# The next unit's first normalisation moved one iteration up, and the kept sums inverted tile by tile

## The reference

```
h = ln(x)*(1+sc)+sh ; windowed self attention (16 heads of 16, windows of 128, rolled by 64) ; x += g*(o @ w_so + b_so)
h = ln(x)*(1+sc)+sh ; scores = q @ k_ctx (77 context rows); top 16 of 77; softmax over them; x += g*(attn @ v @ w_co + b_co)
h = ln(x)*(1+sc)+sh ; u = h @ w_m1 ; x += g*((silu(u[:1024]) * u[1024:]) @ w_m2 + b_m2)
```

```
nx = ln(x)*gamma+beta ; w = softmax(nx @ Wq @ (bank @ Wk).T / 16) ; combined = [nx, w @ (bank @ Wv), anchor]
probs = softmax(combined @ router_W + b) ; 3 experts: silu(combined @ e_w1 + b) @ e_w2 + b, summed with probs
out = x + sigmoid(silu(combined @ gate_w1) @ gate_w2) * (routed @ out_w + out_b)
```

## Time and profile before

| | |
|---|---|
| median of 3 runs | 1451.67 us (1446.48 to 1452.09) |
| the profiled execution | 1447.34 us |
| its span, first to last instruction | 1445.5 us |
| PE busy | 97% of the span |
| DVE busy | 1061.5 us, 73% |
| ACT busy | 815.8 us, 56% |
| POOL busy | 439.9 us, 30% |
| mean granted TensorE clock | 0.992 |

### The profile page before, as it was taken

One profiled execution on the slowest core, in us unless ns is written; L12 is line 12 of the kernel. 1 busy time (PEld: TensorE's weight loads), 2 busy tenths in 40 slices (PEclk: granted clock), 3 DMA queues, 4 the chain that ended last, 5 costly groups with the idle time before them and its releaser, 6 DMA issues.

```text
span 1445.5 us, 29891 instructions
## 1 busy us (share of the span) xinstructions
PE 1402.6 (97%) x9585; PEld 1174.8 (81%) x9585; DVE 1061.5 (73%) x4754; ACT 815.8 (56%) x2523; POOL 439.9 (30%) x600
## 2 busy tenths in 40 slices
PE   7999999999999999999999999999999999999997
PEld 5878788888888788888888788888888878887886
DVE  3576869687786868879696787959688786968632
ACT  3473474747566375755647366564757547474433
POOL 1414132333224233332335132233334313232302
PEclk9999999999999999999999999999999999999999
DMA  7610000000010000010010000000010000000000
GB/s 244 207 64 2 1 8 19 9 27 9 20 32 16 1 2 25 1 34 9 19 33 1 16 1 16 11 23 13 8 34 19 16 2 7 3 1 9 1 2 14
DMA packets 32760, 35.29 MB, mean 24 GB/s; under 512 B 8744, under 2 KB 27868, under 8 KB 32349
## 3 DMA queue, kind: packets, MB, share of 16 engines
q1 hardware_dynamic: 32605, 33.38, 7.6%
HBM read 28.83 MB, written 4.22 MB: 23 GB/s over the span
## 4 chain that ended last, share of the span: by engine, by line
PE 59%; DVE 31%; issue 5%; ACT 2%; POOL 1%; SPq 0%; DMA 0%; DVEq 0%; POOLq 0%; ACTq 0%
PE bank L1033 10%; DVE knocked L2264 10%; PE bank L964 9%; PE bank L1009 7%; PE bank L824 6%; PE bank L1016 4%; DVE M L2257 4%; DVE M L2252 4%; PE bank L873 4%; PE bank L973 3%; PE bank L863 2%; PE bank L810 2%; DVE scores L2272 2%; PE bank L885 2%; DVE gT L2279 2%
## 5 line engine op out<-in xcount | busy, mean ns | idle before, releaser
L964 PE MATMUL bank<-hB,Wm 128*128 128x256 f32 x1024 | 244.0, 384 | 2.2 <-ACT hB L1404 2.2
L964 PEld LDWEIGHTS bank<-hB,Wm 128*128 128x128 f32 x1024 | 191.8, 191 | 33.8 <-issue 7.0
L1009 PE MATMUL bank<-nxT,W1nx 128*128 128x256 f32 x896 | 212.5, 383 | 0.0
L1443 ACT ACTIVATE prob<-bank,rmax 128x128 f32<-128x128 f32 x512 | 179.9, 435 | 28.1 <-DVE rmax L2191 28.1
L1801 POOL TENSOR_TENSOR scores<-scores,M 128x308 f32<-128x308 f32 x128 | 94.8, 741 | 318.4 <-DVE knocked L2264 317.1
L1033 PE MATMUL bank<-W2p,gT 128*128 128x256 f32 x768 | 183.2, 381 | 3.0 <-DVE acc L2343 1.9
L1009 PEld LDWEIGHTS bank<-nxT,W1nx 128*128 128x128 f32 x896 | 166.5, 191 | 23.2 <-issue 2.8
L1033 PEld LDWEIGHTS bank<-W2p,gT 128*128 128x128 f32 x768 | 141.2, 190 | 23.8 <-issue 2.8
L1493 ACT ACTIVATE tbs<-bank,b1half 128x256 f32<-128x256 f32 x128 | 60.6, 473 | 145.0 <-PE bank L964 103.9
L1443 ACT ACTIVATION_READ_ACCUMULATOR prob<-bank,rmax 128x1 f32 x512 | 140.7, 276 | 0.0
L1509 ACT ACTIVATE tbs<-bank,betaH 128x256 f32<-128x256 f32 x224 | 95.1, 486 | 80.1 <-PE bank L1016 79.1
(11 more groups left out here) (240 smaller groups left out, 2800.7 us busy)
## 6 DMA issues: line engine op xcount, KB each, us to landing
Wm_g<-in_L_xcond_w_m_dram SPq DMA_DIRECT2D x4, 1024.0 KB, 5.5
W1ev<-in_L_xcond_e_w_dram SPq DMA_DIRECT2D x6, 512.0 KB, 7.6
x<-in_x_dram SPq DMA_DIRECT2D x16, 128.0 KB, 2.5
x<-in_x_dram SPq DMA_DIRECT2D x32, 64.0 KB, 2.4
Wm<-in_L_xcond_w_m_dram SPq DMA_DIRECT2D x1, 2048.0 KB, 9.2
out_dram<-acc SPq DMA_DIRECT2D x16, 128.0 KB, 1.7
out_dram<-acc SPq DMA_DIRECT2D x32, 64.0 KB, 2.0
batch_rows<-row_store SPq DMA_DIRECT2D x4, 384.0 KB, 3.7
```

Source lines behind the costliest of these rows:

```text
L964: m = pe.matmul(bank_of(name)[:, half * UT:(half + 1) * UT], Wm1[:, k, c:c + P], hB[:, k, :], start=(k == 0), stop=(k == CB - 1))
L1009: pe.matmul(bank_of(name)[:, n * UT:(n + 1) * UT], W1nx[:, k, c0 + n * P:c0 + (n + 1) * P], nxT[:, k, :], start=(n == 0 and k == 0), stop= ...
L1443: m = act.activation(prob[:, s, i, :], psum[s][:, i * P:(i + 1) * P], ACT.Exp, bias=rmax[:, t, s * HPS + i:s * HPS + i + 1], accum_out=rsu ...
```

## The change

Three edits. (1) The first normalisation of the unit that enters stage A in iteration k+1 moves from the first half of that iteration to the end of iteration k, on DVE and on POOL; the first two such units have theirs in the prologue. (2) Sum, inverse and spreading of the kept scores go tile by tile, with pick(1, 0) and the first sum ahead of the last top-16 step; PE waits for each tile's inverses by itself. The query bias comes behind all of them. (3) ACT copies the last picks of tile 0 and exponentiates the kept scores of tile 0 earlier in its list. The `last_cross` iteration gets edits 2 and 3.

```diff
 PE, a_turn_inverses
-                pe.wait_ge(spread if values == "pv" else spread_x, u + 1)
                 wait_free(pe, name, u)
                 bk = bank_of(name)
-                for f in range(CB):
-                    for t in range(1 if values == "pv" and u >= 2 else TILES):
+                if values == "pv":
+                    pe.wait_ge(spread, u + 1)
+                for t in range(1 if values == "pv" and u >= 2 else TILES):
+                    if values == "xv":
+                        pe.wait_ge(spread_x, u * TILES + (t + 1))
+                    for f in range(CB):
 ACT, both (last_cross alike)
                 a_copy_picked(0, 2, c)
+                a_copy_picked(0, 3, c)
                 b_proto_exp(b)
                 a_cross_exp(1, 0, c)
-                a_copy_picked(0, 3, c)
+                a_kept_exp(0, c)
                 a_copy_values(a)
                 b_copy_weights(b)
                 a_cross_exp(1, 1, c)
-                a_kept_exp(0, c)
 POOL
+            def a_spread_kept(t, u):
+
+                pool.wait_ge(kept_inverted, u * TILES + (t + 1))
+                pool.tensor_copy(kept[:, t], kinv[:, t, :].rearrange("p (h a) -> p h a", a=1).to_broadcast([P, H, D])).then_inc(spread_x, 1)
 POOL, both
                 a_shift(0, 1, c)
-                rstd_of(0, EPS0, a)
...
                 a_shift(1, 3, c)
+                a_spread_kept(0, c)
                 a_shift_kept(1, c)
-                a_spread("xv", c)
+                a_spread_kept(1, c)
...
                 rstd_of(2, EPS0, c)
+                if a + 1 < NU:
+                    rstd_of(0, EPS0, a + 1)
                 rstd_of(1, EPS0, a)
 DVE
-            def a_invert_kept(u):
-                dve.wait_ge(kept_sum, u * TILES + TILES)
-                dve.reciprocal(kinv[:, :, :], ksum[:, :, :]).then_inc(kept_inverted, 1)
+            def a_invert_kept(t, u):
+                dve.wait_ge(kept_sum, u * TILES + (t + 1))
+                dve.reciprocal(kinv[:, t, :], ksum[:, t, :]).then_inc(kept_inverted, 1)
 DVE, end of the prologue
+                a_load(2, 0)
+                ln_stats(0, xs[2], 2)
+                wait_full(dve, "ln2", 1)
+                ln_apply(0, xs[2], xnA, 2)
 DVE, both
                     prep_m(batch)
-                a_load(ra, batch)
-                ln_stats(0, xa, a)
                 a_topk("a", 0, 1, c)
...
                 b_swiglu(3, b)
-                wait_full(dve, "ln2", a - 1)
-                ln_apply(0, xa, xnA, a)
                 b_swiglu(4, b)
...
                 a_topk("b", 1, 2, c)
+                a_pick(1, 0, c)
+                a_sum_kept(0, c)
+                a_invert_kept(0, c)
                 a_topk("b", 1, 3, c)
-                a_pick(1, 0, c)
+                a_pick(1, 1, c)
+                a_sum_kept(1, c)
+                a_invert_kept(1, c)
                 a_bias_queries(a)
-                a_pick(1, 1, c)
-                a_sum_kept(0, c)
-                a_sum_kept(1, c)
-                a_invert_kept(c)
                 b_silu("h00", hE[:, 0], 0, b)
...
                 ln_apply(2, xc, xnB, c)
+                if a + 1 < NU:
+                    a_load((r + 2) % UNITS, (a + 1) // UNITS)
+                    ln_stats(0, xn, a + 1)
                 a_values_out(oT, a)
...
                 ln_apply(1, xa, xnA, a)
                 b_mix(2, b)
+                if a + 1 < NU:
+                    wait_full(dve, "ln2", a)
+                    ln_apply(0, xn, xnA, a + 1)
                 b_finish(b, xb)
```

More of the change, by code:

```diff
@@ L1812, in a_spread @@
             def a_spread(values, u):
[L1814 to L1819, removed]
-                alone(pool)
-                for t in range(1 if values == "pv" and u >= 2 else TILES):
-                    i = pool.tensor_copy(each[values][:, t], inv[:, t, :].rearrange("p (h a) -> p h a", a=1).to_broadcast([P, H, D]))
-                i.then_inc(spread if values == "pv" else spread_x, 1)
+                pool.wait_ge(sums_inverted, u + 1)
+                alone(pool)
+                for t in range(1 if u >= 2 else TILES):
+                    i = pool.tensor_copy(each[values][:, t], rinv[:, t, :].rearrange("p (h a) -> p h a", a=1).to_broadcast([P, H, D]))
+                i.then_inc(spread, 1)
+            def a_spread_kept(t, u):
+                pool.wait_ge(kept_inverted, u * TILES + (t + 1))
+                pool.tensor_copy(kept[:, t], kinv[:, t, :].rearrange("p (h a) -> p h a", a=1).to_broadcast([P, H, D])).then_inc(spread_x, 1)
             def gate(w, n, b, done):
@@ L1923, in prologue @@
                 a_spread("pv", 1)
-                a_spread("xv", 0)
+                a_spread_kept(0, 0)
+                a_spread_kept(1, 0)
                 rstd_of(1, EPS0, 1)
                 rstd_of(2, EPS0, 0)
+                rstd_of(0, EPS0, 2)
             def both(k, r, batch):
@@ L2453, in prologue @@
                 a_sum_kept(0, 0)
+                a_invert_kept(0, 0)
                 read_fold("p21", W2p[:, 2 * RB + 2:2 * RB + 4, :].rearrange("p k c -> p (k c)"), fold_psum("p21")[:, :])
@@ L2463, in prologue @@
                 a_sum_kept(1, 0)
-                a_invert_kept(0)
+                a_invert_kept(1, 0)
                 a_normalise("pv", oT, 1)
@@ L2475, in prologue @@
                 ln_apply(2, xs[0], xnB, 0)
+                a_load(2, 0)
+                ln_stats(0, xs[2], 2)
+                wait_full(dve, "ln2", 1)
+                ln_apply(0, xs[2], xnA, 2)
             def both(k, r, batch):
                 a, c, b = k + 1, k, k - 1
-                ra, xa, xc, xb = (r + 1) % UNITS, xs[(r + 1) % UNITS], xs[r], xs[r - 1]
+                xn, xa, xc, xb = xs[(r + 2) % UNITS], xs[(r + 1) % UNITS], xs[r], xs[r - 1]
                 b_swiglu(0, b)
```

## The result

The changed kernel takes 1482.8 us (median of 4 runs, 1479.34 to 1485.38) against 1449.68 for the kernel before (1446.48 to 1452.09): ratio 1.0233 [1.0212, 1.0254], slower by 33 us. The profiled execution took 1479.34 (span 1477.6), 32.0 more than that of before.

A forecast was written before the change was run, and what follows sets the result against it. TensorE was taken to bound the kernel, busy 1402.6 of 1445.5 us. The wait's 12.7 us, with the clock's 12 making 24.6, on the profiled 1447.34 gave 1472 us; range 1456 to 1484.

The forecast's parts named there:

- the forecast's own band: Whole kernel: new PE wait plus clock falls in some iterations, 1466 to 1479 us, chance 0.42.
- rival 2: PE clock falls nearly every time, 12 to 14 falls costing 20 to 24 us: 1480 to 1488; chance 0.1.
- the first term: PE's new wait over 14 iterations: 14 x 1.1 = 15.4, less 3 x 0.8 and 0.3, gives 12.7 us.
- the forecast's 1.1 and 0.3: Added time per iteration from PE's wait ahead of y10: 1.1 us, but net 0.3 at r=3.
- The bank: y10 reuses q's PSUM bank, so the query bias, not the pick, releases PE's turn, about 0.15 us later.
- The size of the delay: On DVE the query bias ends 1.90 us later (1.75 to 2.1); PE idles about 1.85 ahead of y10.
- The normalisation: DVE reaches the mo residual 1.7 us sooner; worth at most about 0.8 per r=3 iteration, 0.3 in all elsewhere.
- the sign of being wrong: Prediction wrong if, among other signs, DVE has no idle at the mo residual; about 1.7 us expected, 1.0 at r=3.
- The clock: PE's idle lowers its clock in half of 14 iterations, 3.4 us each losing about 1.7: 12 us.
- Costed at 0: End-of-iteration stats and apply, POOL's split spread (up to 0.3), ScalarE's list and the last cross iteration: 0 us.

The follow-up runs named there:

- e1: Changed kernel with eight throwaway products put into PE's wait right before its turn of y10; 1461.85 us, ratio 1.0091 against the kernel before.
- e5: Changed kernel with q and v exchanged between PSUM banks 0 and 1, every engine's order kept; 1436.22 us, ratio 0.9907 against the kernel before.
- e3: Kernel before with only the query bias moved behind the kept reciprocal; 1466.09 us, ratio 1.0121.
- e4: Kernel before with only the first normalisation moved to the end of the preceding iteration; 1446.88 us, ratio 0.9979.
- e2: Changed kernel with the query bias put back directly behind pick(1, 0); 1448.68 us, ratio 1.0000 against the kernel before.
- e8: e2 with sum and reciprocal of tile 0 moved behind pick(1, 1); 1491.8 us, ratio 1.0304 against the kernel before.
- e6: e5 with top-16 step b03 ahead of a10, and b03 and pick(0,1) earlier still where r is not 3; 1433.63 us, ratio 0.9884 against the kernel before.
- e7: e6 with the last cross iteration reordered too: residual right behind pick(0,0), a10 behind pick(0,1); 1434.6 us, ratio 0.9889 against the kernel before.
- f2: Kernel before with only q and v exchanged between PSUM banks 0 and 1; 1448.81 us, ratio 1.0006.
- f1: e6 with the early b03 only at r = 1 and 2, r = 0 ordered like r = 3; 1428.29 us, ratio 0.9871 against the kernel before.

## Why the prediction was right, and where it was off

*The number.* 1482.8 lies in the range of 1456 to 1484, near its upper end, but above the forecast's own band of 1466 to 1479. It lies in the band of rival 2 (1480 to 1488), whose condition, 12 to 14 falls, did not hold: 8 of the 14 iterations have one. Of the 32.0 us by which the profiled execution is slower, 12.7 are the wait with its offsets (10.4 in the twelve iterations, 1.25 and 1.06 in iterations 1 and 14), 17.9 the clock, 4.0 lie ahead of iteration 1 and -2.6 behind iteration 14. The forecast had 12.7, 12 and nothing at the ends. That the first term comes out at 12.7 is partly luck: PE's wait is 2.1 us where the forecast had 1.85, and in e1 the iterations with r other than 3 are 0.3 to 1.5 longer than before, not 1.1 each. And 4.0 of the total come from a place that the forecast had at 0.

*The bank.* Right, and shown: e5 takes only the shared bank away, and the slower kernel becomes a faster one; e3 makes only the late bias, and has the wait.

*The size of the delay.* From the start of pick(1,0) to the end of the bias DVE takes 5.34 us in the changed kernel and 1.58 in the earlier trace rows. Of the difference b13, which begins at 258.38, takes with its idle 260.28-258.38 = 1.90, which stood ahead of the pick before; 1.86 is left, against a forecast of 1.90. PE's wait is 2.1 where I had "about 1.85". In e1 the wait costs 10.4 us in twelve iterations; by the forecast's 1.1 and 0.3 it would be 9 x 1.1 + 3 x 0.3 = 10.8.

*The normalisation.* "Worth at most about 0.8 in the three r=3 iterations", and 0.3 elsewhere, 2.7 in all: e4 gave about 3. The size is borne out, the place was not. DVE does not stand idle 1.7 (1.0 at r = 3) ahead of the residual: in the changed kernel it is 0.1 to 0.44 over the 14 iterations, which comes near to the sign of being wrong that I had put down, no idle there. At r = 2 it is 0.34, and 1.20 lies one step earlier, where the last swiglu waits for ScalarE; DVE's timeline at r = 2, then the residual at r = 3:

```profile
238.83 0.43 DVE L2287 SCALAR_TENSOR_TENSOR gT<-tbs,gT 128x256 f32<-128x256 f32 x1 [1.20 <-ACT gT L1498]
...
242.22 0.69 DVE L2247 TENSOR_TENSOR x<-x,bank 128x512 f32<-128x512 f32 x1 [0.34 <-PE bank L976]
...
673.29 0.69 DVE L2247 TENSOR_TENSOR x<-x,bank 128x512 f32<-128x512 f32 x1 [0.17 <-PE bank L976]
```

I had looked for the end of the lead at the step that I knew to be gated, and not at each wait on the way.

*The clock.* The mis-sized term. A stretch costs 1.63 us where I had 1.7, but I took seven of them, and there were eleven, in 8 iterations: 17.9 us against 12. Three of the falls lasted 6.8 us, and I multiplied a number of falls by the price of the shortest. The trace of before had shown the longer kind, outside the iterations (its windows, as in the earlier trace rows):

```profile
98.60:105.40 6.80, 6.75 (x30) 6.20 (x30) 1.54 (x5) 3.75 (x13) 1.48 (x4) 0.50 0.49 154
1334.20:1341.00 6.80, 6.69 (x24) 5.50 (x25) 6.80 (x48) 2.27 (x5) 1.92 (x3) 0.50 0.00 0
```

The clock is 6 of the 11 us by which 1472 is short. Another 3.5 are the median's distance from the profiled execution, the fastest of the four and the one with the highest mean granted clock (0.980, against 0.978, 0.975 and 0.975 in the others). The ends are the rest. The Trainium skill's rule (TensorE: Matmul & The Clock Gate, "Why this matters for your kernels") would have put this term at 0; the traces of the changed kernel and of e3 disagree with it, as falls to a clock of 0.50 came at idle pieces of 2.0 to 2.4 us in the one and of 1.6 in the other, and e1, where the same gap is filled, kept 1.00.

*Costed at 0.* The additions at the end of the iteration, POOL's split, ScalarE's list and the last cross iteration. The end of the span, from iteration 14 on, is 1.5 us shorter than before, but it has one stretch of 3.4 us at half clock (at 1369.6) where before has three (6.8 us at 1334.2 and 3.4 at 1375.2), the last 2 us left aside, which run at half clock in both. In e1, whose end has the same three, it is 2.1 us longer than before, 1.07 of that in iteration 14 with its wait. So about 1 us may have been lost in the last cross iteration or behind it; what took it is open. In the iterations e2 bounds the sum of these terms: with all of them in, and a wait of 1.0 at the picks, its twelve iterations are 2.5 us shorter than before. The cover is thinner than I had said for POOL: e8 shows that the spread of tile 0 ahead of the second kept shift costs 0 only as long as reciprocal 0 comes early.

*Left open.* 4.0 us of the profiled difference lie ahead of iteration 1, with a fall of 6.8 us at 28.2 that the profiled execution of before lacks. The profiled executions of e1, e2, e4, e5, e6, e7 and e8 have such a fall, those of e3, f2 and f1 don't. f1 has the moved normalisation too and has none, so it isn't simply a part of the change; one profile of each, with runs of before itself from 1442.8 to 1452.5, can't settle it. How much the two ends can move shows in e4: three of its ten runs took 1440.3 to 1440.8 us at a mean clock of 0.994, the others 1445.5 to 1448.7 at 0.990 or 0.991. It is also open which of the waits brings a fall, and why some falls are twice as long.

## What to carry to other kernels

Before an instruction that drains a buffer is moved back, look up which job uses that buffer next: the wait view names one releaser, and here the second wait showed only as a constant lag of 0.15 us behind the end of the other instruction. If the order is right and the buffer wrong, exchange the buffers, not the order. Where the bound engine gets a new wait of some 2 us in every iteration, price what it does to the clock as well, with falls of more than one length; here that was the larger part (17.9 us against 10.4 in the twelve iterations).

## What was unexpected

The longer wait brought more than more idle time, as far as one profile of each can tell: about 1.0 us gave no stretch of half clock in the 14 iterations (e2), 1.65 on average gave 5 (e3), 2.1 gave 11 (the change), while filling the gap of 2.1 with eight throwaway products (16 matmul records) gave none and made the kernel 21 us faster than without them (1461.85 against 1482.8). And an in-order queue turned the relief of a wait of 1.0 us into a loss of 43 (e8 against e2).
